# A graph-network layer on one core: the short last chunk of edges summed in the prologue, group 31's x part done there too, and a new order of the last step

## The chip, the cores and the metric

The kernel runs on one core of one Trainium2 chip. The metric is the device time of one execution in microseconds; the median of three runs of the kernel before is 318.07 us (317.57 to 318.27).

## What is computed

```python
agg = segment_sum(edge_attr, dst, num_segments=12500)    # 200000 edges x 128, dst sorted
h = relu(layernorm(x))                                   # 12500 nodes x 128
h = concatenate([h, agg], -1)
h = relu(h @ W1 + b1); h = relu(h @ W2 + b2); h = h @ W3 + b3
out = x + (h - mean(h)) * rsqrt(var(h) + 1e-5) * ln_w + ln_b
```

Everything is float32. The edges alone are 102.4 MB, x and the result 6.4 MB each.

## The kernel before

Edges are sorted by their node. A chunk is 384 edges (3 rows for each of 128 partitions); four chunks are a quad (1536 edges, 768 KB), of which there are 130 (q = 0 to 129). 130 quads leave 320 edges over. They are the short last chunk: it is read as the last 384 edges, and the 64 of them that quad 129 has already counted (`DONE`) are masked out with -1.

For each quad, `seg` (L428) sums the four chunks on PE: 12 matmuls with one-hots of 32 nodes (`onehot`, made for eight chunks at a time by VectorE in `make_onehot`, L876). ScalarE copies the sums from PSUM (`copy_part`, L655), GpSimd makes a placement matrix (`placement`, L795), PE multiplies both (`put`, L444), and VectorE adds the result into `agg` in SBUF at a base read from the data (`add`, L952). Edges come into a ring of eight slots, two loads of 384 KB for each quad, all issued by SP; SP may reload a slot when PE is through with the quad in it (`reload`, L331). Every node group is 384 nodes: groups 0 to 31, and LAST with 212 nodes. A group needs its x part: LayerNorm statistics (`stats_x`, `mean_x`, `scale_x`, `shift_x` on VectorE, `x_sqrt` and `normalise` on ScalarE), three transposes on PE (`transpose_h`), a copy (`copy_ht`); then layer 1 as two matmuls accumulated in one bank (`layer1_x`, `layer1_sums`, the second of which needs the sums), `relu1`, `layer2`, `relu2`, `layer3`; and on VectorE `take_y`, `stats_y`, `mean_y`, `center_y`, `scale_y`, `output`. GpSimd adds the bias into x (`bias_x`).

The order of every engine's instructions is written out by hand. Prologue: dst is loaded, the one-hots' columns are worked out, quads 0 and 1 are summed, group LAST's x part is done, and a flag (L942, L944) decides whether the data fit the windows; while it is worked out PE runs `SPARE` = 20 small matmuls whose results nobody uses (L513). Then every engine branches to `fast`. It does quads 0 to 5 and group 0's x part, and then steps: step i sums four quads (q = 4i + 6 on), does the layers of group i, the x part of group i + 1, and the output of group i - 1. A last step, outside the loops, handles quads 126 to 129, groups 30, 31 and LAST, and the short chunk (L549 to L584 on PE, L738 to L760 on ScalarE, L1089 to L1116 on VectorE). Step 29 does the x part of group 31 too (`more_x`). The x of a group is loaded three steps ahead; results are stored by SP, those of eight groups in parts between the edge loads, those of groups 8 to 29 in pairs behind the last edge load (L328), group 31 by ScalarE's queue (L760), LAST by SP (L315).

## Time and profile before

| | before |
|---|---|
| median of 3 runs | 318.07 us (317.57 to 318.27) |
| the profiled execution | 318.06 us, its span 316.3 us |
| PE busy | 271.3 us, 86% of the span |
| VectorE (DVE) | 248.8 us, 79% |
| GpSimd (POOL) | 168.9 us, 53% |
| ScalarE (ACT) | 149.1 us, 47% |
| DMA | 116.48 MB, mean 368 GB/s |

The span is what the trace covers, from the first instruction to the last; 1.8 us of the execution's time lie outside it. Matmuls are pipelined, so a busy PE is not PE at its peak. "SPq" in a chain is SP's sequencer, which issues the DMAs. All times in the rows are microseconds from the start of the span. A matmul in float32 shows as two records.

### The profile page before, as it was taken

What the parts mean: (1) busy time and instruction counts of PE and PEld (TensorE: products, weight loads), DVE (VectorE), ACT (ScalarE), POOL (GpSimd) and SP (SyncE); (2) the same over time, 40 slices, a digit from 0 to 9 for tenths busy, and PEclk for the clock granted to TensorE, in tenths of its full rate; (3) what the DMA queues carried; (4) which work ended last, traced back from release to release, by engine and by line L of the source; (5) the groups of instructions that cost most, each with busy time, mean ns of one, the idle gap of its engine ahead of it and who ended that gap; (6) DMA issues with size and microseconds to landing.
All of it is one profiled execution on the core that took longest, in us unless ns stands there. A gap on an engine that the chain in (4) does not pass through costs nothing.

```text
span 316.3 us, 12837 instructions
## 1 busy us (share of the span) xinstructions
PE 271.3 (86%) x3967; PEld 185.0 (58%) x3967; DVE 248.8 (79%) x944; ACT 149.1 (47%) x407; POOL 168.9 (53%) x208
## 2 busy tenths in 40 slices
PE   2977999998898888888998888889988888899891
PEld 0654666665565556565665565666655656566460
DVE  4937588988787878878787879788787888877985
ACT  1442555555544445455544444555443545544622
POOL 8626556665545464645545555554446464555431
PEclk9979999999999999999999999999999999999997
DMA  7999999999999999999999999999999999999995
GB/s 246 355 373 372 373 371 372 373 373 373 373 373 373 373 373 373 373 373 373 376 380 378 380 380 379 379 383 379 379 382 378 378 380 383 379 382 381 382 395 180
DMA packets 81854, 116.48 MB, mean 368 GB/s; under 512 B 5712, under 2 KB 81840, under 8 KB 81840
## 3 DMA queue, kind: packets, MB, share of 16 engines
q1 hardware_dynamic: 80826, 115.86, 103.5%
q10 hardware_dynamic: 1014, 0.46, 0.6%
q8 instruction: 6, 0.10, 0.1%
q14 instruction: 8, 0.07, 0.1%
HBM read 109.90 MB, written 6.40 MB: 368 GB/s over the span
## 4 chain that ended last, share of the span: by engine, by line
SPq 52%; PE 16%; issue 13%; DVE 9%; DMA 7%; POOL 1%; DVEq 0%; ACT 0%; POOLq 0%
SPq L296 40%; PE part_ps L439 6%; DMA ring<-in_edge_attr 6%; SPq L323 6%; SPq L291 4%; PE place_ps L450 3%; DVE onehot L880 2%; PE hid_ps L474 2%; PE hid_ps L484 1%; PE hid_ps L467 1%; DMA dst_i<-in_dst 1%; PE y_ps L490 1%; SPq L332 1%; DVE z L999 1%; POOL place L802 1%
## 5 line engine op out<-in xcount | busy, mean ns | idle before, releaser
L802 POOL TENSOR_SCALAR place<-iota,rows_at 128x128 f32<-128x128 f32 x131 | 95.0, 727 | 113.3 <-PE place_ps L450 103.7
L439 PE MATMUL part_ps<-ring,onehot 128*32 128x128 f32 x3120 | 111.9, 277 | 25.7 <-DMA ring<-in_edge_attr 25.7
L439 PEld LDWEIGHTS part_ps<-ring,onehot 128*32 128x32 f32 x3120 | 77.4, 109 | 71.1 <-issue 51.5
L958 DVE TENSOR_TENSOR agg<-place_ps,agg 128x128 f32 x131 | 38.1, 291 | 48.3 <-PE place_ps L450 46.3
L880 DVE TENSOR_TENSOR onehot<-iota,local_t 128x768 f32<-128x768 f32 x66 | 66.2, 1004 | 0.2 <-issue 0.2
L450 PE MATMUL place_ps<-place,part 128*128 128x128 f32 (+1 forms) x262 | 63.6, 325 | 2.7 <-POOL place L802 2.2
L810 POOL TENSOR_TENSOR xs<-xs,vecs 128x384 f32 (+2 forms) x33 | 53.8, 1632 | 19.3 <-ACT h L671 19.3
L657 ACT ACTIVATE part<-part_ps 128x128 f32<-128x128 f32 x131 | 34.8, 267 | 47.0 <-PE part_ps L439 45.1
L450 PEld LDWEIGHTS place_ps<-place,part 128*128 128x128 f32 (+1 forms) x262 | 39.1, 188 | 29.1 <-issue 21.4
L671 ACT ACTIVATE h<-xs,x_shift,x_rstd 128x128 f32 (+2 forms) x98 | 41.3, 483 | 2.4 <-DVE x_shift L873 2.4
L687 ACT ACTIVATE hid<-hid_ps,b1s 128x384 f32<-128x384 f32 (+1 forms) x33 | 19.0, 576 | 44.8 <-PE hid_ps L474 44.8
L1017 DVE SCALAR_TENSOR_TENSOR xs<-z,y_rstd,xs 128x128 f32 (+1 forms) x93 | 31.0, 385 | 4.1
L663 ACT ACTIVATE x_std<-x_mv,eps 128x3 f32<-128x3 f32 (+1 forms) x33 | 9.8, 297 | 42.9 <-DVE x_mv L861 42.9
L490 PE MATMUL y_ps<-w3s,hid 128*128 128x128 f32 x192 | 29.7, 291 | 0.0
L680 ACT ACTIVATE h_t<-ht_ps 128x384 f32<-128x384 f32 x32 | 22.3, 697 | 14.0 <-PE ht_ps L459 14.0
L999 DVE SCALAR_TENSOR_TENSOR z<-y,y_mv,vecs 128x128 f32<-128x128 f32 x96 | 28.4, 348 | 0.1
L484 PE MATMUL hid_ps<-hid,w2s 128*128 128x384 f32 (+1 forms) x66 | 26.8, 487 | 0.5 <-ACT hid L687 0.5
L467 PE MATMUL hid_ps<-h_t,w1x 128*128 128x384 f32 x64 | 26.1, 489 | 0.8 <-ACT h_t L680 0.8
L474 PE MATMUL hid_ps<-agg,w1a 128*128 (+2 forms) x66 | 26.5, 483 | 0.0
L490 PEld LDWEIGHTS y_ps<-w3s,hid 128*128 128x128 f32 x192 | 23.8, 191 | 1.3 <-issue 0.5
L853 DVE BATCH_NORM_STATS2 x_stats<-xs 128x6 f32 (+2 forms) x98 | 22.0, 279 | 0.8 <-DVE flag_i L944 0.8
L983 DVE BATCH_NORM_STATS2 y_stats<-y 128x6 f32<-128x128 f32 x96 | 20.8, 272 | 0.1
(88 smaller groups left out, 206.1 us busy)
## 6 DMA issues: line engine op xcount, KB each, us to landing
ring<-in_edge_attr SPq DMA_DIRECT2D x260, 384.0 KB, 9.0
xs<-in_x SPq DMA_DIRECT2D x32, 192.0 KB, 8.5
out_x<-xs SPq DMA_DIRECT2D x11, 384.0 KB
out_x<-xs SPq DMA_DIRECT2D x16, 72.0 KB
dst_i<-in_dst SPq DMA_DIRECT2D x1, 768.0 KB
out_x<-xs SPq DMA_DIRECT2D x8, 48.0 KB
ring<-in_edge_attr SPq DMA_DIRECT2D x1, 192.0 KB, 8.7
out_x<-xs SPq DMA_DIRECT2D x1, 192.0 KB
```

The costliest lines, as they stand in the source:

```text
L296: sp.dma_start(ring_slot(slot)[:, k * HALF:(k + 1) * HALF, :], half_of_edges(q, k)).then_inc(edges_loaded[slot], 16)
L439: last = nc.tensor.matmul(part_ps[par_q % 2][s * WIN:(s + 1) * WIN, 0:D], onehot[:, oct_par, first + s, j, :], e[:, s, j * D:(j + 1) * D], ...
L450: nc.tensor.matmul(place_ps[par_q % 2][:, 0:P], part[0:rows, par_q % 2, :], place[0:rows, par_q % 2, :], start=True, stop=True).then_inc(p ...
L474: nc.tensor.matmul(hid1_ps[:, 0:n], w1a[:, :], agg[:, bass.ds(g * CHUNK, n)], start=False, stop=True).then_inc(hid1_done, 1)
L490: last = nc.tensor.matmul(y_ps[:, j * D:(j + 1) * D], hid2[:, j, :], w3s[:, :], start=True, stop=True)
L657: nc.scalar.activation(part[0:rows, par_q % 2, :], part_ps[par_q % 2][0:rows, 0:D], ACT.Copy).then_inc(part_copied, 1)
L671: last = nc.scalar.activation(h[0:rows, j, :], xg(g, j), ACT.Relu, bias=x_shift[0:rows, j:j + 1], scale=x_rstd[0:rows, j:j + 1])
L802: nc.gpsimd.tensor_scalar(place[:, par_q % 2, :], iota[:, 0:P], rows_at[:, k:k + 1], None, ALU.is_equal).then_inc(place_ready, 1)
L810: nc.gpsimd.tensor_tensor(v, v, lnbs[0:rows, :].unsqueeze(1).to_broadcast([rows, per, D]), ALU.add).then_inc(x_biased, 1)
L880: nc.vector.tensor_tensor(onehot[:, par % 2, :, :, :], iota[:, 0:WIN].unsqueeze(1).unsqueeze(1).to_broadcast([P, OCT, PER, WIN]), local_t[ ...
L958: nc.vector.tensor_tensor(v, place_ps[par_q % 2][:, 0:P], v, ALU.add).then_inc(added, 1)
L999: last = nc.vector.scalar_tensor_tensor(z_of(g, j), y_of(g, j), y_mv[0:rows, j, 0:1], lnws[0:rows, :], ALU.subtract, ALU.mult)
```

## The change

The short chunk has tiles and semaphores of its own. Its destinations are loaded once more, one edge per element (`tail_i`); its edges go to `tail_e`, behind the first loads of x and ahead of quads 1 to 7. VectorE makes them relative to node 12372 (`TAIL_BASE`), masks the edges that quad 129 counts, and makes a one-hot of 128 nodes for each of its three rows. After the branch PE sums it with three dense matmuls straight into `place_ps[1]`, and VectorE adds it into `agg`. PE waits for that add ahead of quad 2. The separate last segment, copy, placement, put, add and one-hot go.

Group 31 (`TOP`) has its x loaded in the prologue too and its x part done there: statistics ahead of the flag, scale and shift behind it, its three activations on ScalarE ahead of the branch, transposes on PE behind put(0), the copy to `h_top_t` behind copy_part(1), the bias on GpSimd ahead of group 0's. `more_x` goes from step 29.

In the last step the order of PE, ScalarE and VectorE is new; LAST's layer 1 uses the bank `ht_ps`, so it need not wait for the bank of group 31. `SPARE` is 15.

```diff
-SPARE = 20
+SPARE = 15
@@ SP, prologue
+                sp.dma_start(tail_i[:, :], dst[TAIL0:EDGES].rearrange("(p j) -> p j", j=PER)).then_inc(tail_dst_loaded, 16)
...
                 load_x(0, 0, 0)
+                sp.dma_start(xg(TOP), group_rows(x, TOP)).then_inc(top_x_loaded, 16)
                 load_x(1, 1, 0)
+                sp.dma_start(tail_e[:, :, :], edges[TAIL0:EDGES, :].rearrange("(p j) f -> p j f", j=PER)).then_inc(tail_loaded, 16)
@@ SP, end
-                    sp.wait_ge(seg_done, QUADS - RING + 1)
-                    tail = QUADS % RING
-                    sp.dma_start(ring[:, tail, 0:PER * D],
-                                 edges[TAIL0:EDGES, :].rearrange("(p j) f -> p (j f)", j=PER)).then_inc(edges_loaded[tail], 16)
@@ PE
+        def layer1_bank(g):
+            return ht_ps if isinstance(g, int) and g == LAST else hid1_ps
...
                 def fast():
                     pe.wait_ge(wts_loaded, WTS)
+                    pe.wait_ge(tail_loaded, 16)
+                    pe.wait_ge(tail_onehot_ready, 1)
+                    for j in range(PER):
+                        last = nc.tensor.matmul(place_ps[1][:, 0:P], tail_e[:, j, :], tail_onehot[:, j, :],
+                                                start=(j == 0), stop=(j == PER - 1))
+                    last.then_inc(tail_summed, 1)
                     for q in range(AHEAD):
+                        if q == 2:
+                            pe.wait_ge(tail_added, 1)
                         if q >= 2:
                             pe.wait_ge(part_copied, q - 1)
                             seg(q, q, LANDED, q // 2 + 1)
                         if q >= 1:
                             put(q - 1, q - 1, free=q >= 3)
+                        if q == 1:
+                            transpose_h(TOP)
                     transpose_h(0)
...
-                    layer1_x(g)
+                    put(q - 1, q - 1)
+                    layer1(g, q - 1)
                     seg(q, q, loads_of(q), q // 2 + 1)
-                    put(q - 1, q - 1)
-                    layer1_sums(g, q - 1)
+                    layer2(g)
                     put(q, q)
-                    transpose_h(g + 1)
                     seg(q + 1, q + 1, loads_of(q + 1))
-                    layer2(g)
+                    layer1_x(TOP)
                     put(q + 1, q + 1)
-                    layer1_x(g + 1)
                     seg(q + 2, q + 2, loads_of(q + 2), q // 2 + 2)
                     layer3(g)
                     put(q + 2, q + 2)
                     seg(q + 3, q + 3, loads_of(q + 3))
-                    layer1_sums(g + 1, QUADS - 1)
+                    layer1_sums(TOP, QUADS - 1)
                     put(q + 3, q + 3)
-                    slot = QUADS % RING
-                    pe.wait_ge(onehot_ready, QUADS // 2 + 1)
-                    pe.wait_ge(edges_loaded[slot], loads_of(QUADS) - LANDED + 16)
-                    for j in range(PER):
-                        last = nc.tensor.matmul(part_ps[QUADS % 2][0:WIN, 0:D], onehot[:, (QUADS // 2) % 2, 0, j, :],
-                                                ring[:, slot, j * D:(j + 1) * D], start=(j == 0), stop=(j == PER - 1))
-                    last.then_inc(seg_done, 1)
-                    layer2(g + 1)
                     layer1_x(LAST)
-                    put(QUADS, QUADS, rows=WIN)
+                    layer2(TOP)
+                    layer1_sums(LAST, QUADS)
+                    layer3(TOP)
+                    layer2(LAST)
                     layer3_last_bias()
-                    layer3(g + 1)
-                    layer1_sums(LAST, QUADS + 1)
-                    layer2(LAST)
                     layer3_last()
@@ ScalarE
                 x_sqrt(LAST)
                 normalise(LAST)
+                x_sqrt(TOP)
                 copy_ht(LAST)
+                normalise(TOP)
 
                 def fast():
                     act.wait_ge(wts_loaded, WTS)
                     for q in range(2):
                         copy_part(q, q)
+                    copy_ht(TOP)
                     x_sqrt(0)
                     normalise(0)
...
+                    relu1(g)
                     copy_part(q, q)
-                    relu1(g)
-                    copy_ht(g + 1)
+                    relu2(g)
                     copy_part(q + 1, q + 1)
-                    relu2(g)
                     y_sqrt(g - 1)
                     copy_part(q + 2, q + 2)
                     copy_part(q + 3, q + 3)
                     relu1(g + 1)
                     y_sqrt(g)
-                    copy_part(QUADS, QUADS, rows=WIN)
                     relu2(g + 1)
                     relu1(LAST)
                     relu2(LAST)
@@ GpSimd
                     for q in range(2):
                         placement(q, q, q, 1, free=False)
+                    bias_x(TOP)
                     bias_x(0)
@@ VectorE, prologue
                 dve.wait_ge(local_t_ready, ROWT)
+                dve.wait_ge(tail_dst_loaded, 16)
+                nc.vector.tensor_scalar(tail_local[:, :], tail_i[:, :], float(TAIL_BASE), None, ALU.subtract).then_inc(tail_rebased, 1)
                 whole = DONE // PER
-                nc.vector.memset(local_t[0:whole, DONE % PER:PER, CHUNKS:CHUNKS + 1], -1.0)
-                nc.vector.memset(local_t[0:whole + 1, 0:DONE % PER, CHUNKS:CHUNKS + 1], -1.0).then_inc(tail_masked, 1)
+                dve.wait_ge(tail_rebased, 1)
+                nc.vector.memset(tail_local[0:whole, DONE % PER:PER], -1.0)
+                nc.vector.memset(tail_local[0:whole + 1, 0:DONE % PER], -1.0).then_inc(tail_masked, 1)
+                dve.wait_ge(tail_masked, 1)
+                nc.vector.tensor_tensor(tail_onehot[:, :, :], iota[:, 0:P].unsqueeze(1).to_broadcast([P, PER, P]),
+                                        tail_local[:, :].unsqueeze(2).to_broadcast([P, PER, P]), ALU.is_equal
+                                        ).then_inc(tail_onehot_ready, 1)
+                stats_x(TOP, top_x_loaded, 16)
+                mean_x(TOP)
...
+                scale_x(TOP)
+                shift_x(TOP)
...
                     shift_x(0)
                     dve.wait_ge(base_ready, 1)
                     dve.wait_ge(agg_zeroed, 1)
+                    dve.wait_ge(tail_summed, 1)
+                    v = agg[:, TAIL_BASE:NODES]
+                    nc.vector.tensor_tensor(v, place_ps[1][:, 0:P], v, ALU.add).then_inc(tail_added, 1)
+                    dve.wait_ge(tail_added, 1)
                     base = bases(0, AHEAD - 1)
@@ VectorE, last step
                     center_y(g - 1)
-                    make_onehot(q // 2 + 2, 1)
                     add(q + 1, q + 1, base[2])
                     scale_y(g - 1)
                     output(g - 1)
+                    take_y(g)
                     add(q + 2, q + 2, base[3])
-                    take_y(g)
                     stats_y(g)
                     mean_y(g)
+                    add(q + 3, q + 3, base[4])
                     center_y(g)
                     scale_y(g)
-                    add(q + 3, q + 3, base[4])
                     output(g)
-                    add(QUADS, QUADS, base[5])
```

## Rows read from the trace of the kernel before

**Rows 1.** The page: the chain's shares by line; issues of edge loads, us to landing.

```profile
SPq L296 40%; PE part_ps L439 6%; DMA ring<-in_edge_attr 6%; SPq L323 6%; SPq L291 4%; PE place_ps L450 3%; DVE onehot L880 2%; PE hid_ps L474 2%; PE hid_ps L484 1%; PE hid_ps L467 1%; DMA dst_i<-in_dst 1%; PE y_ps L490 1%; SPq L332 1%; DVE z L999 1%; POOL place L802 1%
...
ring<-in_edge_attr SPq DMA_DIRECT2D x260, 384.0 KB, 9.0
```

**Rows 2.** Stretches: us, busy PE, PEld, DVE, ACT, POOL; PE clock, DMA share, GB/s.

```profile
20.00:30.00 10.00, 7.68 (x158) 5.89 (x155) 5.88 (x16) 3.70 (x11) 6.24 (x10) 0.93 1.06 372
240.00:280.00 40.00, 35.39 (x532) 24.07 (x533) 31.62 (x120) 18.29 (x50) 21.27 (x26) 1.00 1.06 380
310.00:317.00 7.00, 0.69 (x4) 0.48 (x4) 2.96 (x13) 1.39 (x6) 1.28 (x3) 0.61 0.32 110
```

**Rows 3.** Timeline of PE, step 29: start, us, instruction, idle before and its releaser.

```profile
285.29 0.86 PE L439 MATMUL part_ps<-ring,onehot 128*32 128x128 f32 x24 [0.93 <-DMA ring<-in_edge_attr]
```

**Rows 4.** Timeline of SP's queue, the last loads and the stores in pairs.

```profile
284.07 0.37 SPq L291 DMA_DIRECT2D xs<-in_x  x1
...
291.27 0.94 SPq L296 DMA_DIRECT2D ring<-in_edge_attr  x2
292.43 0.48 SPq L357 DMA_DIRECT2D ring<-in_edge_attr  x1
292.96 11.00 SPq L328 DMA_DIRECT2D out_x<-xs  x11
```

**Rows 5.** Timeline of the last step up to quad 129: group 31's x part and the tail's one-hot.

```profile
293.81 0.67 DVE L853 BATCH_NORM_STATS2 x_stats<-xs 128x6 f32<-128x128 f32 x3
...
295.71 1.26 ACT L671 ACTIVATE h<-xs,x_shift,x_rstd 128x128 f32<-128x128 f32 x3 [0.44 <-DVE x_shift L873]
...
297.19 0.30 PEld L450 LDWEIGHTS place_ps<-place,part 128*128 128x128 f32 x2 [1.03 <-ACT part L657]
...
300.40 1.04 DVE L880 TENSOR_TENSOR onehot<-iota,local_t 128x768 f32<-128x768 f32 x1
```

**Rows 6.** Timeline from quad 129's segment to VectorE's last instructions.

```profile
302.32 0.86 PE L439 MATMUL part_ps<-ring,onehot 128*32 128x128 f32 x24
...
303.23 0.91 PE L474 MATMUL hid_ps<-agg,w1a 128*128 128x384 f32 x2
...
304.18 0.58 ACT L687 ACTIVATE hid<-hid_ps,b1s 128x384 f32<-128x384 f32 x1 [0.66 <-PE hid_ps L474]
...
304.30 0.84 PE L574 MATMUL part_ps<-ring,onehot 128*32 128x128 f32 x6
...
305.07 0.91 PE L484 MATMUL hid_ps<-hid,w2s 128*128 128x384 f32 x2
...
306.02 0.58 ACT L693 ACTIVATE hid<-hid_ps,b2s 128x384 f32<-128x384 f32 x1 [0.58 <-PE hid_ps L484]
...
307.12 0.94 PE L490 MATMUL y_ps<-w3s,hid 128*128 128x128 f32 x6
...
308.09 0.56 DVE L963 TENSOR_TENSOR y<-y_ps,vecs 128x384 f32<-128x384 f32 x1 [0.91 <-PE y_ps L490]
...
312.46 0.72 DVE L1017 SCALAR_TENSOR_TENSOR xs<-y,y_last_rstd,xs 106x128 f32<-106x128 f32 x2
```

**Rows 7.** Timeline of the prologue: spares, the flag's input, copy_part(0), quad 2, put(2).

```profile
18.91 2.34 PE L513 MATMUL hid_ps<-ident 128*32 128x32 f32 x40
19.15 0.28 DVE L942 TENSOR_REDUCE worst<-place_ps 1x1 f32<-1x128 f32 x1 [2.13 <-PE place_ps L510]
...
20.29 0.45 ACT L657 ACTIVATE part<-part_ps 128x128 f32<-128x128 f32 x2 [1.29 <-DVE flag_i L944]
...
21.78 0.86 PE L439 MATMUL part_ps<-ring,onehot 128*32 128x128 f32 x24
...
26.05 0.46 PE L450 MATMUL place_ps<-place,part 128*128 128x128 f32 x2 [2.20 <-POOL place L802]
```

**Rows 8.** Stretches of 1 us in the prologue, columns as in rows 2.

```profile
18.00:19.00 1.00, 1.00 (x6) 0.62 (x7) 0.00 (x0) 0.36 (x1) 0.72 (x1) 0.51 1.07 373
25.00:26.00 1.00, 0.00 (x0) 0.00 (x0) 0.69 (x2) 0.00 (x0) 1.00 (x2) 1.00 1.06 373
```

## What the change should do, worked out from the rows

> **What bounds the kernel now.** I read the page's chain first: 40% of the span is the SP queue issuing edge loads [rows 1]. Two things can look like that: SP too slow, or SP held back by full DMA queues. The stretches decide it: from 20 us on the DMA share stays at 1.06 and the rate at 372 to 380 GB/s [rows 2], and an edge load lands 9.0 us (median) after its issue [rows 1], far longer than 384 KB at 380 GB/s (1.03 us) takes. So about 9 us of transfers always stand in the queues, and bytes set the pace. PE agrees: deep in the loop it waits 0.93 us for a ring slot once a step [rows 3]; it is close behind, not the limit. The bytes are the same in both kernels but for 1.5 KB. So time can only be won at the end: by when the last quad (q=129) is summed, and by how long the chain behind it is.
>
> At the end the loads are no longer the last thing. Quad 129's two loads are issued from 291.27 to 292.21 [rows 4]; with the median 9.0 us for the second (issued about 291.75) they have landed by about 300.8. PE starts quad 129 at S = 302.32 [rows 6], 1.5 us later. The rows just before tell why: VectorE is full (one-hots, group 31's statistics), ScalarE is busy 1.26 us with group 31's h, so PE waits 1.03 us for a copied part at 297.19 [rows 5]. I call that time "late at S". After S comes a serial chain: sums matmul of group 31 at 303.23, its relu, layer 2 at 305.07 (behind the tail chunk's six matmul records from 304.30), relu 2 at 306.02, layer 3 at 307.12, VectorE's take_y at 308.09, then LayerNorm of group 31 and of LAST in one row on VectorE, whose last instructions run from 312.46 to 313.18 [rows 6]; the last stores take the 3.1 us from there to the end of the span.
>
> **Part 1, bytes ahead of quad 129.** The tail chunk's 192 KB were issued behind quad 129 (292.43 [rows 4]) and now go ahead of all quads but the first: 0.197 MB / 380 GB/s = +0.52 us on its landing. Group 31's x was ahead of it before too (284.07 [rows 4]) and stays ahead: 0. The new load of tail_i is 128 pieces of 12 bytes on SP's queue, ahead of quad 0. No row shows such a load by itself. Lower bound 0 (it hides behind the 768 KB of dst already queued), upper bound 0.48 us, the whole issue of the tail chunk's 128 longer pieces [rows 4]; I take 0.1. The Trainium skill's page "DMA: Bandwidth & Descriptors" (Specifications) puts pieces under 512 B at less than line rate because they are read, modified and written; it gives no time for 128 of them, the sum does not use it. Landing of quad 129: 300.8 + 0.52 + 0.1 = 301.4.
>
> **Part 2, what leaves the last steps.** From VectorE: stats of group 31 0.67, its means about 0.3, two small ones about 0.35, the one-hot for the tail chunk 1.04 [rows 5], one add 0.3: 2.6 us out of a stretch where it was nearly full. From ScalarE: 1.26 for h and a transposed copy of about 0.7. From PE: three transposes and the tail chunk. From GpSimd: one placement. What is late next? Not VectorE (2.6 us of slack against the 1.5 it was behind), but the DMA again: quads arrive every 2.07 us (0.786 MB / 380) and PE needs 1.2 plus one layer, at most 1.9. So quad 129 starts when it has landed or when PE is through layer 3 of group 30, both near 301.4 to 301.6. I take S' = 301.57: 0.75 us earlier than 302.32. Bounds: 0 (PE still late) and 0.9 (start at 301.4).
>
> **Part 3, the chain after S.** Before: take_y at S + 5.77. After, with the same durations: quad 0.79, so group 31's sums at S'+0.81 (the wait for the add of quad 128 that put them at S+0.91 goes); relu 1 0.95 later, as now (303.23 to 304.18): 1.76, ends 2.34; layer 2 at 2.38. Before it came at S+2.75 as the tail chunk stood in front. Now put(129), 0.42, and LAST's x matmul, 0.36, fit before 2.38. Relu 2 at +0.95 (305.07 to 306.02): 3.33, ends 3.91; LAST's sums run meanwhile on PE, done by 3.4, if the add of quad 129 is there: put(129) ends about 1.9, the add 2.2, so 0.8 us of slack. Layer 3 at 3.95, take_y at +0.97: 4.92. That is 0.85 less than 5.77 [rows 6]. From take_y to the end VectorE's order is unchanged (5.09 us, 308.09 to 313.18). LAST must be ready for it: its relu 1 follows relu 2 of group 31, layer 2 follows layer 3, layer 3 of LAST is done about S'+6.6, and VectorE wants it at 4.92 + 2.7 = 7.6: hidden with 1.0 us to spare; if that cover goes, each us later is a us on the end. center_y, scale_y and output of group 30 now stand behind the add of quad 129: 1.9 us on VectorE from S'+2.3, over at 4.2, before take_y at 4.92. The bounds of this part: 0 (some relu or the LAST path late by as much) and 1.2 (relus earlier).
>
> **Part 4, the prologue.** New on VectorE ahead of the flag: rebase, two memsets, a one-hot of 384 elements (half of the 1.04 us for 768), stats 0.67 and means 0.3: about 1.9 us. VectorE idles 2.13 us there before `worst` [rows 7], so the flag moves by 0 to 0.3. After the flag, ScalarE must first make h of TOP: x_sqrt at 19.4, VectorE's scale and shift to 20.0, three activations 1.26 to 21.3. So copy_part(0), at 20.29 before, starts about 21.4. Behind it on ScalarE are queued copy_part(1) and copy_ht(TOP), which waits for PE's put(0) and the transposes (22.7), then x_sqrt(0) about 23.5. VectorE waits for that in scale_x(0), and the tail's add is queued behind: about 24.5. PE waits for the add ahead of quad 2, which thus starts about 24.7 against 21.78 [rows 7]. But before, PE lost 2.20 us at 26.05 waiting for GpSimd's placement [rows 7]; this moves only as far as h of group 0, about 1.7 us, so by quad 4 PE is 1 to 2 us later than now. That costs nothing while the queues are fed. Quads 8 and 9 need only quads 0 and 1; the bytes issued by 24 us (9.6 MB, now 10.0) less those moved (the slices give about 7.8) leave 2.2 MB or 5.8 us of backlog when SP comes to wait for quad 2, done 25.5. SP waits about 1.5 us, the backlog falls to 4 us. The cover is gone only if quad 2 is more than about 5 us late; then each us is one us of the end.
> The five spare matmuls less free 5/20 of 2.34 us = 0.6 us of PE [rows 7], three dense matmuls take it back (0.4 to 1.3 us): nothing, as PE then waits for copy_part(0).
> TensorE's clock: granted 0.51 at 18 us, after PE had stood still from about 15.4 to 18.0, the lower level, 1.2 GHz; yet the idle stretch of 24 to 26 us left it at 1.00 [rows 8]. The new gap (22.8 to 24.7) resembles the second. The Trainium skill, "TensorE: Matmul & The Clock Gate", section "HAM oscillation — how this bites in real kernels", says that an idle PE that waits for its data is throttled again and begins its next work cold. By that rule quads 2 to 5 would run at 1.2 GHz. From rows: twice 0.86 us each, some 3.5 us more PE lag, which by the backlog above still ends near 0 us of cost, at worst 1.
>
> **The sum.** 0.75 (S) + 0.85 (chain) = 1.6 us. The profiled execution took 318.06 us with a span of 316.3, the median is 318.07: 318.06 - 1.6 = 316.5.
>
> **The rivals.**
> *A: only one of the two gains.* For it: landing and PE are near each other at S', and the queues are not empty at the end: 310 to 317 still has a DMA share of 0.32 [rows 2], some 2.2 us of full work, of which the three last stores are only a part. If LAST's stores, now issued at 311.6, find the stores of finished groups in front, they end about 0.8 us later than I say; so too if the loads start 0.8 us later. 318.06 - 0.8 = 317.3, up to 317.8. Against it: SP's last store of two groups is issued by 303.96 [rows 4], 7.6 us ahead.
> *B: slower, the queues run dry in the prologue.* Mechanism: SP cannot reload until quad 2 is summed; ScalarE's copy_part(0) and x_sqrt(0) stand behind TOP, and the cold clock stretches what follows. It decides once SP's wait exceeds the 5.8 us of backlog, less the roughly 2 us in which PE has to get quads 2 to 4 away. If it does, some 3 to 4 us of stream are lost against the 1.6 won: 319.5. For it: a serial loop ScalarE, PE, ScalarE, VectorE, PE that did not exist. Against: 4 us of cover left by my reckoning.
> *C: more is won.* PE may start right on landing and the relus come sooner (bounds 0.9 + 1.2 = 2.1), or quads land sooner than the median says: 315.7.
> *D: nothing changes.* The end is bound by the stream and its stores to the last byte: 318.0. Against: LAST's stores are issued long after the last backlog is thin.
>
> **How the numbers follow.** Forecast (316.1 to 317.1) 0.58; A 0.18; C 0.11; B 0.08; D 0.05. Likeliest: 316.5. The range leaves out B and half of C's far side: 315.5 to 318.1. About 0.2% (0.64 us) is what a measurement can tell from no change: faster than 317.43 is the forecast, C and a third of A: 0.75; slower than 318.71 is B: 0.08; between 0.17.
>
> **What would show it.** Right: quad 129's segment starts 0.6 to 0.9 us earlier and waits for the DMA or for nothing; take_y of group 31 starts 4.7 to 5.2 us behind it; quad 2 starts near 24.7 while the DMA share stays at 1.06 in 20 to 30 us; VectorE's `worst` at 19.1 to 19.5. Wrong: a slice at 20 to 35 us under 370 GB/s (B); the last store landing over 3.2 us after VectorE's last instruction (A); quad 129 starting after 302 with a wait for a part or an add before it (part 2); PE at 0.5 clock beyond 25 us. The prediction fails most easily at part 2, where S' rests on a median landing.

## The result and the profile after

The ratio is 0.9979, 95% interval 0.9969 to 0.9989: 0.7 us faster, 0.35 to 1.0. The forecast was 316.5, 1.6 us faster: the sign was right, the size more than twice too large, and 317.63 lies inside the range.

The page's chain by line answers to [rows 1]:

```profile
SPq L324 46%; DMA ring<-in_edge_attr 6%; SPq L353 6%; PE part_ps L471 5%; SPq L319 5%; PE place_ps L482 2%; DMA dst_i<-in_dst 1%; PE hid_ps L515 1%; PE hid_ps L498 1%; SPq L362 1%; PE hid_ps L505 1%; PE y_ps L521 1%; DVE onehot L916 1%; DVE local L940 1%; DVE least L938 1%
```

SP's issues of edge loads take still more of it, 46% for 40%, and VectorE's one-hots 1% for 2%. The stretches of its trace (us, busy PE, PEld, DVE, ACT, POOL, PE clock, DMA share, GB/s) answer to [rows 2]:

```profile
20.00:30.00 10.00, 6.95 (x126) 5.15 (x129) 5.15 (x17) 4.12 (x14) 6.56 (x10) 1.00 1.06 372
240.00:280.00 40.00, 34.61 (x510) 23.39 (x508) 31.63 (x123) 18.43 (x51) 22.48 (x28) 1.00 1.06 380
310.00:311.00 1.00, 0.00 (x0) 0.00 (x0) 0.85 (x6) 0.67 (x3) 0.10 (x1) 1.00 0.83 298
311.00:312.00 1.00, 0.00 (x0) 0.00 (x0) 0.93 (x5) 0.51 (x3) 1.00 (x3) 0.50 0.42 158
312.00:313.00 1.00, 0.00 (x0) 0.00 (x0) 0.58 (x2) 0.00 (x0) 0.17 (x1) 0.50 0.18 61
```

The stream is as full as before, and the queues are nearly empty when the last stores are issued. The timeline of the prologue answers to [rows 7]: the flag's input, the spares, copy_part(0), quad 2, put(2).

```profile
18.28 1.11 PE L544 MATMUL hid_ps<-ident 128*32 128x32 f32 x30
...
18.53 0.24 DVE L987 TENSOR_REDUCE worst<-place_ps 1x1 f32<-1x128 f32 x1
...
20.55 0.41 ACT L692 ACTIVATE part<-part_ps 128x128 f32<-128x128 f32 x2
...
23.20 0.86 PE L471 MATMUL part_ps<-ring,onehot 128*32 128x128 f32 x24 [1.53 <-DVE agg L1088]
...
26.69 0.46 PE L482 MATMUL place_ps<-place,part 128*128 128x128 f32 x2 [1.41 <-issue]
```

The timeline of the end answers to [rows 3, 4 and 6]: quad 122, the last edge loads on SP, quad 129, and the chain behind it.

```profile
286.75 0.86 PE L471 MATMUL part_ps<-ring,onehot 128*32 128x128 f32 x24 [0.80 <-DMA ring<-in_edge_attr]
...
292.00 1.06 SPq L324 DMA_DIRECT2D ring<-in_edge_attr  x2
...
302.57 0.86 PE L471 MATMUL part_ps<-ring,onehot 128*32 128x128 f32 x24
...
303.36 0.91 PE L505 MATMUL hid_ps<-agg,w1a 128*128 128x384 f32 x2
...
304.31 0.58 ACT L721 ACTIVATE hid<-hid_ps,b1s 128x384 f32<-128x384 f32 x1 [0.54 <-PE hid_ps L505]
...
304.94 0.91 PE L515 MATMUL hid_ps<-hid,w2s 128*128 128x384 f32 x2
...
305.89 0.58 ACT L727 ACTIVATE hid<-hid_ps,b2s 128x384 f32<-128x384 f32 x1 [0.82 <-PE hid_ps L515]
...
306.53 0.94 PE L521 MATMUL y_ps<-w3s,hid 128*128 128x128 f32 x6 [0.31 <-ACT hid L727]
...
307.50 0.56 DVE L1010 TENSOR_TENSOR y<-y_ps,vecs 128x384 f32<-128x384 f32 x1 [0.80 <-PE y_ps L521]
...
311.77 0.81 DVE L1064 SCALAR_TENSOR_TENSOR xs<-y,y_last_rstd,xs 106x128 f32<-106x128 f32 x2
```

What the reader is to see: take_y of group 31 is 4.93 us behind quad 129's start, where the forecast said 4.92, and VectorE's end is 5.08 us behind that. But quad 129 starts at 302.57, not 301.57, which is later than the 302.32 of before. And there is no wait for the DMA at it. The trace also has the landing of each quad's second load. For quad 122, then for quad 129, the view of the line that issues them gives the start of the issue and the time from there to the landing:

```profile
L324 SPq DMA_DIRECT2D ring<-in_edge_attr x1: 939/939/939, 277.2 to 277.2; - x1
DMA to landing us min/median/max: 9.5/9.5/9.5
...
L324 SPq DMA_DIRECT2D ring<-in_edge_attr x1: 597/597/597, 292.5 to 292.5; - x1
DMA to landing us min/median/max: 9.0/9.0/9.0
```

Quad 122 landed at 277.2 + 9.5 = 286.7 and PE began it at 286.75, at once. Quad 129 landed at 292.5 + 9.0 = 301.5, where the forecast said 301.4, and PE came to it 1.1 us later. (In the profile of before the same view gives 291.8 + 8.8 = 300.6 for quad 129, 1.7 us ahead of its start.)

Only two waits of PE show between quad 122 and quad 129: the 0.80 us for quad 122, and 0.55 us for group 30's h_t. That suggested another theory, called T below: the last thing that PE waits for from the stream is quad 122, the first quad of step 29, behind an x load; from there on PE works off what it has. Then bytes ahead of quad 122 cost time and bytes between quads 122 and 129 cost none. Theory R is the forecast's: the landing of quad 129 counts.

### The profile page after: what moved, and what is told of

It reads as the page before. It is cut to its first block, busy times and chain, and to the rows that moved or that the text cites. A ratio compares the mean times of both kernels' runs of the same rounds, so it can differ in the third digit from the quotient of the medians.

```text
span 315.5 us, 12788 instructions
## 1 busy us (share of the span) xinstructions
PE 272.2 (86%) x3955; PEld 184.7 (59%) x3955; DVE 244.4 (77%) x945; ACT 148.9 (47%) x406; POOL 167.5 (53%) x206
## 4 chain that ended last, share of the span: by engine, by line
SPq 59%; issue 13%; PE 12%; DMA 7%; DVE 6%; ACT 1%; DVEq 0%; ACTq 0%
SPq L324 46%; DMA ring<-in_edge_attr 6%; SPq L353 6%; PE part_ps L471 5%; SPq L319 5%; PE place_ps L482 2%; DMA dst_i<-in_dst 1%; PE hid_ps L515 1%; PE hid_ps L498 1%; SPq L362 1%; PE hid_ps L505 1%; PE y_ps L521 1%; DVE onehot L916 1%; DVE local L940 1%; DVE least L938 1%
## 5 line engine op out<-in xcount | busy, mean ns | idle before, releaser
L482 PE MATMUL place_ps<-place,part 128*128 128x128 f32 x260 | 62.9, 324 | 1.7 <-issue 1.4
L844 POOL TENSOR_TENSOR xs<-xs,vecs 128x384 f32 (+2 forms) x33 | 52.5, 1591 | 21.1 <-ACT h L706 21.1
L916 DVE TENSOR_TENSOR onehot<-iota,local_t 128x768 f32<-128x768 f32 x65 | 62.4, 962 | 1.5 <-issue 0.2
L482 PEld LDWEIGHTS place_ps<-place,part 128*128 128x128 f32 x260 | 38.9, 188 | 27.5 <-issue 20.1
L721 ACT ACTIVATE hid<-hid_ps,b1s 128x384 f32<-128x384 f32 x32 | 18.6, 580 | 44.4 <-PE hid_ps L505 44.4
L1064 DVE SCALAR_TENSOR_TENSOR xs<-z,y_rstd,xs 128x128 f32 (+1 forms) x93 | 27.9, 353 | 6.5 <-DVE y_rstd L1054 6.4
L714 ACT ACTIVATE h_t<-ht_ps 128x384 f32<-128x384 f32 x31 | 21.6, 696 | 13.6 <-PE ht_ps L491 13.6
L515 PE MATMUL hid_ps<-hid,w2s 128*128 128x384 f32 (+1 forms) x66 | 26.7, 486 | 0.1
L505 PE MATMUL hid_ps<-agg,w1a 128*128 (+1 forms) x64 | 26.0, 488 | 0.0
L498 PE MATMUL hid_ps<-h_t,w1x 128*128 128x384 f32 x62 | 25.2, 489 | 0.6 <-ACT h_t L714 0.6
```

What stands on the lines that cost most here:

```text
L482: nc.tensor.matmul(place_ps[par_q % 2][:, 0:P], part[0:rows, par_q % 2, :], place[0:rows, par_q % 2, :], start=True, stop=True).then_inc(p ...
L505: nc.tensor.matmul(layer1_bank(g)[:, 0:n], w1a[:, :], agg[:, bass.ds(g * CHUNK, n)], start=False, stop=True).then_inc(hid1_done, 1)
L515: nc.tensor.matmul(hid2_ps[:, 0:n], w2s[:, :], hid1[:, 0:n], start=True, stop=True).then_inc(hid2_done, 1)
L844: nc.gpsimd.tensor_tensor(v, v, lnbs[0:rows, :].unsqueeze(1).to_broadcast([rows, per, D]), ALU.add).then_inc(x_biased, 1)
L916: nc.vector.tensor_tensor(onehot[:, par % 2, :, :, :], iota[:, 0:WIN].unsqueeze(1).unsqueeze(1).to_broadcast([P, OCT, PER, WIN]), local_t[ ...
```

## Landmarks of all the profiles

The columns, in us: start of quad 122 (it waits for the DMA in every kernel), from there to the start of quad 129, from there to take_y of group 31, VectorE's end, and from that to the end of the span. The last columns are the median, and the ratio to the kernel before on the same chip with its interval.

| kernel | quad 122 | to 129 | to take_y | DVE end | to span end | median | ratio |
|---|---|---|---|---|---|---|---|
| before | 285.29 | 17.03 | 5.77 | 313.18 | 3.1 | 318.04 | |
| e11 before again | 286.19 | 16.35 | 5.71 | 313.34 | 3.4 | 318.19 | 1.0005 (0.9992 to 1.0018) |
| e1 before, x31 early | 286.07 | 16.36 | 5.72 | 313.23 | 3.1 | 318.79 | 1.0017 (1.0003 to 1.0030) |
| e10 before, x31 behind q4 | 285.78 | 16.34 | 5.74 | 312.94 | 3.1 | 318.89 | 1.0025 (1.0012 to 1.0038) |
| e6 before, both early | 286.63 | 16.35 | 5.71 | 313.78 | 3.3 | 320.31 | 1.0061 (1.0041 to 1.0081) |
| the changed kernel | 286.75 | 15.82 | 4.93 | 312.58 | 2.9 | 317.63 | 0.9979 (0.9969 to 0.9989) |
| e2 no tail_i load | 286.66 | 15.79 | 4.93 | 312.46 | 3.2 | 317.46 | 0.9980 (0.9965 to 0.9996) |
| e4 parts behind | 286.90 | 15.80 | 4.93 | 312.71 | 3.2 | 317.61 | 0.9990 (0.9974 to 1.0006) |
| e9 loads later | 286.92 | 15.79 | 4.94 | 312.73 | 3.0 | 317.64 | 0.9991 (0.9977 to 1.0005) |
| e3 stored early 6 | 286.17 | 15.79 | 4.94 | 311.98 | 3.9 | 317.76 | 0.9987 (0.9971 to 1.0003) |
| e8 stored early 7 | 287.30 | 15.79 | 4.93 | 313.11 | 3.3 | 317.41 | 0.9975 (0.9962 to 0.9988) |
| e12 stores between | 286.61 | 15.79 | 4.93 | 312.42 | 3.6 | 317.75 | 0.9981 (0.9962 to 1.0000) |
| e5 x31 late | 287.00 | 16.58 | 5.22 | 313.88 | 2.9 | 318.38 | 1.0001 (0.9986 to 1.0017) |
| e7 spare 100 | 288.97 | 15.79 | 4.94 | 314.78 | 2.8 | 319.71 | 1.0047 (1.0024 to 1.0070) |

The columns "to 129" and "to take_y" repeat to 0.06 us in kernels with the same code there, but for the 17.03 of before, to which e11 comes back. The column "quad 122" does not: it differs by 0.9 us between the two executions of the kernel before. The eight kernels with the change's own last step need 15.8 us from quad 122 to quad 129, whatever is in the stream.

## The experiments

**e1: group 31's x moved into the prologue, alone.**

```diff
+                sp.dma_start(xg(GROUPS - 1), group_rows(x, GROUPS - 1)).then_inc(top_x_loaded, 16)
                 load_x(1, 1, 0)
...
-                            stats_x(i + 2, x_loaded[par], 16 * pairs + 32)
+                            stats_x(i + 2, top_x_loaded, 16)
```

> The kernel before with one edit: group 31's x (192 KB) is loaded in the prologue instead of between quads 125 and 126. Theory T (what sets the start of quad 129 is the landing of quad 122, the last one PE waits for, plus PE's and VectorE's own work): every first quad of a step lands 0.52 us later (0.197 MB / 380 GB/s), quad 122 starts near 285.8 instead of 285.29, and the time rises by 0.3 to 0.5 us. Theory R (the forecast's: only the bytes ahead of quad 129 count, and they are the same): quad 129 lands as before, the time is the same within 0.1 us.

Measured: 1.0017 (1.0003 to 1.0030), 0.5 us slower (0.1 to 1.0). The forecast gave this edit the price 0; the low end of the interval only just excludes that, and e10 below excludes it clearly. The profile's quad 122 agrees in direction only, since its 0.78 us contain the spread of the stream. Early in the stream the price is seen better: quad 7 lands at 26.2 us in both profiles of the kernel before, at 26.7 here, at 26.9 in e10. The same load further back in the prologue (**e10**, behind quad 4) costs 0.8 us (0.4 to 1.2), no less:

> The kernel before with group 31's x loaded in the prologue, behind quad 4, where the earlier experiment had it ahead of quad 1. Theory H: without the hole it costs its bytes only, 0.52 us on every quad behind it (deep in the loop 141.3 against 140.8; the earlier placement gave 141.60 in its profile), and the time is 318.4 to 318.6. If any added load in the prologue costs 0.8 us or more wherever it stands, the time is 318.8 or more as there.

**e4: three stores taken out from between quads 122 and 129.**

```diff
-                    step(2 * t + 1, 1, t, g, {0: 0, 3: 1})
-                    step(2 * t + 2, 0, t + 1, g, {2: 2}, more_x=False)
+                    step(2 * t + 1, 1, t)
+                    step(2 * t + 2, 0, t + 1, more_x=False)
+                    for k in range(len(OUT_PARTS)):
+                        store_part(g, k)
```

> The changed kernel with the three stores of group 7 moved from between the loads of quads 122 and 129 to behind quad 129. Only bytes between those two quads move. Theory T: quad 122 lands as in the changed kernel (286.75), quad 129 starts as there (302.57, within 0.15), the time is the same within 0.1 us. Theory R: quad 129 starts 0.52 us earlier and the time falls by 0.5 us.

Measured: the same time (317.61 against 317.63). The rows of PE, quad 122 and quad 129:

```profile
286.90 0.86 PE L473 MATMUL part_ps<-ring,onehot 128*32 128x128 f32 x24 [0.97 <-DMA ring<-in_edge_attr]
...
302.70 0.86 PE L473 MATMUL part_ps<-ring,onehot 128*32 128x128 f32 x24
```

15.80 us apart, as in the changed kernel, though 197 KB fewer stand ahead of quad 129. Quad 129 had landed at 301.3, 1.4 us ahead of its start. That is what T says and R denies.

**e3, e8: two groups' stores, or one, behind the last edge load.** The edit is `STORED_EARLY` = 6, or 7, for 8.

> The changed kernel with STORED_EARLY = 6: the stores of two groups (393 KB) go behind the last edge load instead of into the stream. Theory T: quad 122 lands 1.03 us earlier (near 285.7), quad 129 starts 1.0 us earlier (near 301.55), and VectorE ends 1.0 us earlier; the stores then drain 1.0 us later, near 312.3, so the end gains only 0.5 to 1.0 us: 316.7 to 317.1 us. If the end were bound by the drain of the stores already, the time would not fall. If PE's lag from the prologue were the limit, quad 122 would not move.

> The changed kernel with STORED_EARLY = 7: one group's store leaves the stream. With 6 quad 122 came 0.58 us earlier and VectorE ended 0.60 us earlier, yet the drain of the stores, full until 311.0 and at 0.7 of share until 313.0, held the last stores. With 7: quad 122 near 286.45, VectorE's end near 312.3, and the drain ends near 312.3. If VectorE's end and the drain both bound the end, this lies between: 317.3 to 317.6, at best 0.3 us under the changed kernel; if only the chain bound it, 6 would have gained 0.6 us, which it did not.

With 6, VectorE ends at 311.98, 0.6 us earlier than in the changed kernel, and none of it arrives: 317.76. The 1 us stretches of e3's end, against those of the changed kernel above:

```profile
310.00:311.00 1.00, 0.00 (x0) 0.00 (x0) 0.81 (x6) 0.90 (x4) 0.70 (x2) 1.00 1.03 384
311.00:312.00 1.00, 0.00 (x0) 0.00 (x0) 0.95 (x4) 0.00 (x0) 0.57 (x2) 1.00 0.70 250
312.00:313.00 1.00, 0.00 (x0) 0.00 (x0) 0.00 (x0) 0.00 (x0) 0.00 (x0) 0.95 0.74 262
```

The queues are full until 311, and from VectorE's end to the end of the span it takes 3.9 us instead of 2.9: LAST's stores find others in front. With 7 the time is 317.41, which its interval does not set apart from the changed kernel. The two groups' stores also took only 0.6 us off quad 122's start in the profile, where 393 KB at 380 GB/s would be 1.03.

That price was too high, as the trace of before shows without any experiment. Between quads 50 and 58 no store stands in the stream, between quads 114 and 122 the three parts of one group do. PE waits for the stream at each of the four. The starts of quads 50 and 114, to be read with the 140.81 of quad 58 and the 285.29 of quad 122:

```profile
122.89 0.86 PE L439 MATMUL part_ps<-ring,onehot 128*32 128x128 f32 x24 [1.00 <-DMA ring<-in_edge_attr]
...
267.22 0.86 PE L439 MATMUL part_ps<-ring,onehot 128*32 128x128 f32 x24 [0.94 <-DMA ring<-in_edge_attr]
```

17.92 us without the stores, 18.07 with them. From quad 74 to quad 122, with six groups stored, eight quads take 18.09 us in the mean. So a group's 197 KB among the loads cost 0.15 to 0.17 us, a third of the 0.52 that they would take at 380 GB/s; the rate of the stream is 380 GB/s with the stores in it and 372 without [rows 2]. Two groups' stores are worth 0.3 to 0.4 us, not 1.03. From quad 58 to quad 122, which takes out what the early stream loses in one execution and not in another, it is 144.3 to 144.6 us in the eleven profiles with eight groups stored early 144.1 in e3 and e8, 144.3 in e12 below: less by a few tenths, as two stores or one would be, and not by 1.0.

**e12: the same two groups' stores moved between quads 125 and 128**, where T says that they are free.

```diff
+                    step(2 * t + 1, 1, t)
+                    store(IN_PARTS)
+                    store(IN_PARTS + 1)
...
+                        if k == 1:
+                            store(IN_PARTS + 2)
```

> The changed kernel with the stores of groups 5, 6 and 7 issued between the loads of quads 125 and 128, where PE is behind the stream anyway; the other five stay in parts ahead of quad 122, and the order behind quad 129 is unchanged. Two groups' stores (393 KB) thus leave the stream ahead of quad 122 without coming behind quad 129. Theory T: quad 122 starts 0.6 to 1.0 us earlier than the changed kernel's 286.8 (mean of four profiles), near 286.0; quad 129 lands up to 1.0 us later after it but PE needs 15.8 us to reach it in any case, so it starts near 301.9; the drain ends where it does in the changed kernel; the time falls by 0.4 to 0.7 us, to 316.9 to 317.2. Theory R (bytes ahead of quad 129 set the end): quad 129 starts as in the changed kernel, 317.6. If the later landing of quads 126 to 129 takes PE's slack of 0.8 us, the gain is under 0.3 us and PE waits for a ring slot after quad 125.

Half right. 590 KB now stand between quads 122 and 129 and PE still takes 15.79 us with no wait for a ring slot: T's main claim holds. Quad 129 lands at 302.0 and starts at 302.40, so 0.4 us of its cover are left. But the gain did not come: 317.75. Quad 122 started at 286.61, 0.2 us earlier than the mean of the changed kernel's four profiles and not 0.6 to 1.0: two groups' stores out of the stream are worth 0.3 to 0.4 us, as reckoned above. And the last stores took 3.6 us, against 2.9 to 3.2 in those four, with a DMA share of 0.98, 0.62 and 0.38 from 310 to 313 us. That the drain of the stores took back what was left is likely; one profile does not show it, and e3 shortens the chain and lengthens the drain at once.

T has a limit. In the changed kernel quad 125 lands at 283.6 + 9.5 = 293.1 and starts at 293.10, with nothing to spare, while quads 126 to 129 land 1.1 to 1.7 us ahead of their starts. The stores of e12 were put behind the loads of quad 125. Bytes ahead of that quad were not tried and would hardly be free.

**e2: no load of tail_i; e9: the two new loads later.** In e2 a memset stands for the load. In e9 group 31's x stands behind quad 2 and the short chunk's edges behind quad 4:

```diff
                 for q in range(1, RING):
                     load_quad(q, q)
+                    if q == 2:
+                        sp.dma_start(xg(TOP), group_rows(x, TOP)).then_inc(top_x_loaded, 16)
+                    if q == 4:
+                        sp.dma_start(tail_e[:, :, :], edges[TAIL0:EDGES, :].rearrange("(p j) f -> p j f", j=PER)).then_inc(tail_loaded, 16)
```

> The changed kernel without the load of tail_i (128 pieces of 12 bytes); the tile is filled by a memset instead, so the short chunk is summed into the wrong node. If this load is what holds the stream back by the 0.3 us that bytes do not explain (first quads of a step start 1.35 us later than before, 1.03 us of it are the two 192 KB loads), they start 0.3 us earlier than in the changed kernel (near 141.85 instead of 142.16) and the time falls by 0.3 us. If the load is hidden behind dst, as the forecast had it (0.1 us), nothing moves by more than 0.1 us.

> The changed kernel with its two new 192 KB loads issued later in the prologue: group 31's x behind quad 2, the short chunk's edges behind quad 4. The bytes ahead of quad 122 are the same. Theory H: beyond their bytes (1.03 us) the early loads cost the stream a hole near 13 to 15 us, in which the DMA share falls to 0.8 to 0.9 while SP is held up in an issue; with the loads later the hole is gone (share 1.05 or more in every us from 12 to 20), quads deep in the loop start near 141.85 and the time falls by 0.3 to 0.6 us, to 317.0 to 317.3. If only bytes count, the quads start as in the changed kernel's profile (142.1 to 142.3) and the time stays at 317.6.

Neither moved the time (317.46 and 317.64) nor quad 122 by more than 0.2 us. So the 128 small pieces cost nothing that can be seen, and theory H, a loss by the place of the loads, is not borne out: e9 has no hole (share 1.05 or more from 12 to 18 us) and starts deep in the loop at 142.50, no earlier. What remained of the 1.35 us is taken up by the next run.

**e11: the kernel before once more.**

> The kernel before once more, unchanged, for the spread of its profile and its time. All theories: the ratio is 1.000 within 0.002. If the profile of before is typical, there is no hole in the DMA share at 12 to 16 us and quads deep in the loop start at 140.8 within 0.2; if holes come and go in every kernel, they start up to 1 us later and part of the 1.35 us that the changed kernel's are late is no effect of the change.

The ratio is 1.0005. Quad 58 in the profile of before, then in that of e11:

```profile
140.81 0.86 PE L439 MATMUL part_ps<-ring,onehot 128*32 128x128 f32 x24 [1.00 <-DMA ring<-in_edge_attr]
```

```profile
141.88 0.86 PE L439 MATMUL part_ps<-ring,onehot 128*32 128x128 f32 x24 [0.98 <-DMA ring<-in_edge_attr]
```

The same code, 1.07 us apart, though e11 has no hole at 12 to 16 us either. The landings tell where it arose: quad 7 lands at 26.2 us in both, quad 10 0.4 us later in e11, quad 22 at 60.1 in before and 61.1 in e11. So the stream gains or loses up to 1 us between 26 and 61 us, and the 1.35 us cannot be told from its 1.03 us of bytes and this spread. A second thing differs. VectorE's one-hot of step 29, in before and in e11:

```profile
292.13 1.75 DVE L880 TENSOR_TENSOR onehot<-iota,local_t 128x768 f32<-128x768 f32 x1
```

```profile
293.00 0.95 DVE L880 TENSOR_TENSOR onehot<-iota,local_t 128x768 f32<-128x768 f32 x1
```

In before it ran beside GpSimd's bias_x and took 0.8 us longer. In e11 it ran beside it too, and there GpSimd took 0.8 us longer. The bias in before, then in e11:

```profile
292.05 1.02 POOL L810 TENSOR_TENSOR xs<-xs,vecs 128x384 f32 x1 [0.28 <-ACT h L671]
```

```profile
292.95 1.85 POOL L810 TENSOR_TENSOR xs<-xs,vecs 128x384 f32 x1 [0.31 <-ACT h L671]
```

 From quad 122 to quad 129 it takes 17.03 us there and 16.34 to 16.36 in the four other profiles of this code. So 0.7 us of what [rows 5] show as "VectorE is full" belongs to that one execution. In the changed kernel the same pair meets, and there too GpSimd pays:

```profile
293.51 1.85 POOL L844 TENSOR_TENSOR xs<-xs,vecs 128x384 f32 x1 [0.31 <-ACT h L706]
293.56 0.94 DVE L916 TENSOR_TENSOR onehot<-iota,local_t 128x768 f32<-128x768 f32 x1
```

That the two engines got into each other's way is my reading of the times, one of the two 0.8 us longer each time they meet; no run kept them apart.

**e5: the changed kernel with group 31's x part late again.**

```diff
                     layer2(g)
                     put(q, q)
+                    transpose_h(TOP)
                     seg(q + 1, q + 1, loads_of(q + 1))
...
-                    step(STEPS - 2, 1, (STEPS - 2) // 2)
+                    step(STEPS - 2, 1, (STEPS - 2) // 2, more_x=True)
```

> The changed kernel with its second part undone: group 31's x is loaded in step 28 again, its x part is done by VectorE and ScalarE in step 29, its transposes and copy in the last step; the short chunk stays in the prologue and the last step keeps its new order. Theory T: first quads of a step start 0.5 to 0.8 us earlier than in the changed kernel (near 141.5), quad 122 near 286.1. From there to quad 129 it takes between 16.2 us (PE's 15.8 and three transposes) and the 17.0 of the kernel before: quad 129 starts between 302.3 and 303.1, the chain behind it is the changed kernel's 4.93 us to take_y, and the time is 317.3 to 318.2. If moving group 31's x part is what pays, the time is above the changed kernel's 317.6 by 0.3 us or more; if its bytes cost what its work saves, the two are the same.

318.38, ratio 1.0001 (0.9986 to 1.0017): the short chunk in the prologue and the new order alone win nothing that can be told from zero; with group 31's x part moved too it is 0.9979. Theory T's numbers were missed here: quad 122 started at 287.00, not near 286.1, quad 129 at 303.58, to take_y it took 5.22 and not 4.93, and the time is above the 317.3 to 318.2 stated. Part of the difference shows in the columns: 16.58 and 5.22 against 15.8 and 4.93, 1.1 us, less the 0.5 of its bytes. Why the stream was late, and why to take_y is 0.3 longer here, stays open.

**e6: both loads early, nothing else.**

```diff
+                sp.dma_start(xg(GROUPS - 1), group_rows(x, GROUPS - 1)).then_inc(top_x_loaded, 16)
                 load_x(1, 1, 0)
+                sp.dma_start(tail_e[:, :, :], edges[TAIL0:EDGES, :].rearrange("(p j) f -> p j f", j=PER)).then_inc(tail_loaded, 16)
```

> The kernel before with both 192 KB loads (group 31's x, the short chunk's edges) issued in the prologue where the change has them, and nothing else moved. Theory T: quad 122 starts where the changed kernel has it (286.5 to 286.9 against 285.29), and the time rises by 1.0 to 1.4 us, to 319.1 to 319.5; so the change's other parts together save 1.5 to 1.9 us, what the forecast said, and the place of the loads takes back 1.0 or more. If the loads' place costs little, the time stays below 318.6 and the forecast's savings were too large instead.

1.0061 (1.0041 to 1.0081): 1.3 to 2.6 us slower, from six executions, of which the profiled one was the fastest (318.86 against 319.85 to 320.41). More than the 1.03 us of bytes; the profile, 286.63 at quad 122, does not show the rest. Direction and order agree with T, the surplus stays open; so the price of early bytes is known in time only roughly (0.5, 0.8, and 1.3 to 2.6 us for two loads).

**e7: quad 2 five us later.** The edit is `SPARE` = 100.

> The changed kernel with SPARE = 100: 170 more small matmul records (37 ns each in the changed kernel's profile, 6.3 us) ahead of the branch, so quad 2 starts 4 to 6 us later than the 23.20 us of the changed kernel. By the forecast's reckoning of 5.8 us of queued transfers, SP's waits for quads 2 to 4 are still covered: the DMA share stays at 1.06 in 24 to 34 us, the first quads of a step deep in the loop start as before (142.2), and the time is the same within 0.2 us. By the rival that the queues run dry, there is a hole in the share at 26 to 34 us, and each us of it is one us of the time: 318.5 or more.

```profile
28.17 0.86 PE L471 MATMUL part_ps<-ring,onehot 128*32 128x128 f32 x24 [1.52 <-DVE agg L1088]
```

```profile
29.00:30.00 1.00, 1.00 (x30) 0.85 (x26) 0.50 (x2) 0.38 (x2) 0.75 (x1) 1.00 0.90 315
30.00:31.00 1.00, 0.24 (x12) 0.00 (x0) 1.00 (x1) 0.28 (x1) 1.00 (x2) 1.00 0.93 247
31.00:40.00 9.00, 8.36 (x140) 5.63 (x140) 4.79 (x17) 2.90 (x8) 4.33 (x8) 1.00 1.03 355
```

The rival was right here. Quad 2 came 5.0 us later than in the changed kernel, the queues ran partly dry from 29 us on (355 GB/s for nine us where 372 is normal), quad 122 came 2.2 us later and the time rose by 2.1 us to 319.71. The cover is about 5.0 - 2.2 = 2.8 us for this kernel, an estimate, with the spread of quad 122's start in it; the backlog in bytes came to 5.8 us, and rival B, which took 2 us off it, was nearer with 3.8. The bytes do not account for all of it: from 29 to 40 us e7 moves 342 GB/s where the changed kernel moves 372, 0.33 MB or 0.9 us of stream, while quad 58 comes 2.5 us later. Backlog counted in bytes over all 16 engines is too kind; what became of the other 1.6 us is not shown.

More of the change, by code:

```diff
@@ L45 @@
 DONE = CHUNKS * CHUNK - TAIL0
+TAIL_BASE = NODES - P
 OCT = 2 * QC
@@ L48 @@
 LAST = GROUPS
+TOP = GROUPS - 1
 LAST0 = GROUPS * CHUNK
@@ L98, in gnn_kernel @@
         place = sb("place", [P, 2, P])
+        tail_e = sb("tail_e", [P, PER, D])
+        tail_i = sb("tail_i", [P, PER], I32)
+        tail_local = sb("tail_local", [P, PER])
+        tail_onehot = sb("tail_onehot", [P, PER, P])
         iota = sb("iota", [P, BANK])
@@ L245, in nth, with transposed @@
         def nth(g):
-            return 1 if isinstance(g, int) and g == LAST else g + 2
+            if isinstance(g, int) and g >= TOP:
+                return 1 if g == LAST else 2
+            return g + 3
+        def transposed(g):
+            if isinstance(g, int) and g >= TOP:
+                return h_last_t if g == LAST else h_top_t
+            return h_t
+        def layer1_bank(g):
+            return ht_ps if isinstance(g, int) and g == LAST else hid1_ps
         def group_rows(t, g):
@@ L465, in layer1_x @@
                     pe.wait_ge(ht_ready, nth(g))
-                    t = h_t if n == CHUNK else h_last_t
-                    nc.tensor.matmul(hid1_ps[:, 0:n], w1x[:, :], t[:, :], start=True, stop=False)
+                    nc.tensor.matmul(layer1_bank(g)[:, 0:n], w1x[:, :], transposed(g)[:, :], start=True, stop=False)
                 def layer1_sums(g, sums=None):
@@ L714, in fast, with step @@
                     copy_ht(0)
-                    def step(i, first=False, more_x=False):
+                    def step(i, first=False):
                         q = 4 * i + AHEAD
@@ L763, in general @@
                     act.wait_ge(wts_loaded, WTS)
-                    with act.Fori(0, GROUPS) as g:
+                    copy_ht(TOP)
+                    with act.Fori(0, TOP) as g:
                         x_sqrt(g)
@@ L771, in general @@
                         y_sqrt(g)
-                    relu1(LAST)
-                    relu2(LAST)
-                    y_sqrt(LAST)
+                    for g in (TOP, LAST):
+                        relu1(g)
+                        relu2(g)
+                        y_sqrt(g)
                 branch(act, fast, general)
@@ L840, in general @@
                 def general():
-                    with pool.Fori(0, GROUPS) as g:
+                    bias_x(TOP)
+                    with pool.Fori(0, TOP) as g:
                         bias_x(g)
@@ L1046, in fast, with step @@
                     add(4, 4, base[4])
-                    def step(i, par, pairs, first=False, more_x=False):
+                    def step(i, par, pairs, first=False):
                         make_onehot(2 * i + 4, 0)
@@ L1162, in group @@
                         finish(g)
-                    with dve.Fori(0, GROUPS // 2) as t:
+                    with dve.Fori(0, TOP // 2) as t:
                         group(2 * t, 0, t)
                         group(2 * t + 1, 1, t)
+                    group(TOP - 1, 0, TOP // 2)
+                    finish(TOP)
                     finish(LAST)
```

60 lines of the change are left out of this document (34 added, 26 removed).

## The prediction, point by point

**Part 2 failed, and with it the sum.** "What is late next? Not VectorE, but the DMA again": wrong. The landing of quad 129 came where the forecast had it, 301.5 for 301.4; that PE would be there to meet it did not. From quad 122 on PE needs 15.8 us to reach quad 129 (seven segments of 0.79, seven placements of 0.42, the layers, the wait for h_t), while the stream needs 301.5 - 286.7 = 14.8: taking stores out ahead of it (e4) or putting more in (e12) changes nothing. The term that was mis-sized is PE's time for a quad, "1.2 plus one layer, at most 1.9" against the 2.07 of the stream. The starts of quads 122 to 129 lie 2.51, 1.86, 1.98, 3.88, 1.85, 1.86 and 1.88 us apart: the 3.88 hold the transposes of group 30, the 0.55 us wait for its h_t and both matmuls of its layer 1. And PE is late already at the start of the stretch, as it waits for quad 122; it has to be compared with the stream over the whole stretch. S' came out as 302.57 for 301.57, and that 1.0 us is what the forecast's 1.6 had too much.

**Part 1: right in bytes, wrong in place.** The short chunk's 0.52 us fits its bytes. "Group 31's x stays ahead: 0" is right for quad 129 and wrong for quad 122, behind which it used to stand: another 0.52 us by its bytes. e1 and e10 price it at 0.5 and 0.8 us. The load of tail_i costs nothing visible (e2: 317.46 against 317.63). The Trainium skill, "DMA: Bandwidth & Descriptors" (Specifications), has pieces under 512 B below line rate; no row here shows that for the 128 pieces of tail_i.

**"Late at S" by 1.5 us** was read from one execution, in which 0.7 us were its own. What the removed work and the new order gave back between quads 122 and 129 is 16.35 - 15.80 = 0.55 us. The forecast had the lateness fall from 1.5 us to under 0.2.

**Part 3 was right**: 4.93 for 4.92, and 5.08 to VectorE's end.

**Part 4**: the flag came no later (`worst` at 18.53, before 19.15), quad 2 started at 23.20, earlier than the 24.7 forecast, because copy_part(0) began at 20.55, not 21.4. The cost of nothing is consistent with the changed kernel's full stream, and the cover was overrated (e7). TensorE's clock was granted in full in this profile from 20 to 24 us, 2.4 GHz (first row); in e4, whose prologue is the same code, it was at 0.50, that is 1.2 GHz (second):

```profile
20.00:24.00 4.00, 2.36 (x36) 1.73 (x35) 1.56 (x9) 2.81 (x9) 2.10 (x3) 1.00 1.06 373
```

```profile
20.00:24.00 4.00, 2.69 (x11) 2.30 (x11) 1.40 (x9) 1.96 (x8) 2.19 (x4) 0.50 1.06 374
```

In e4 it stayed there until 30 us, quads 2 to 4 took 1.5 us each for 0.86, quad 2 came 1.0 us later (24.23), and the time was the same (317.61 against 317.63). But it fell at 20 us, ahead of the gap of which the forecast spoke and behind PE's stillness from 16.0 to 17.9. In e2 it was full until 24.6, behind that gap (PE stood from 21.7 to 23.2), and then 0.50 until 31 us, again at no cost in time (317.46). The rule of the Trainium skill, "TensorE: Matmul & The Clock Gate", section "HAM oscillation — how this bites in real kernels", that an idle PE begins its next work cold, thus fits e2 and not the changed kernel's own profile.

**The rivals.** A, only one of the two gains, is what happened (317.3 was its time): the chain gained 0.8 us, S' nothing. Its own reasons, late loads or stores in front of LAST's, are not what took S' away. Whether the forecast's 316.5 would have come with S' at 301.57 was not tested: VectorE would have ended at 311.6, where the changed kernel's DMA share is still 0.42, and in e3, which ends at 312.0 with more stores behind it, the last stores took 3.9 us instead of 2.9. B did not happen, but decides at about 2.8 us. C is out. D was wrong for this kernel; whether it holds for a further shortening of the chain is open for the same reason.

**The sum by what was measured**: bytes ahead of quad 122 +1.03, from there to quad 129 -0.55, to take_y -0.8, the rest 0: -0.3 us. The medians differ by 0.41, the ratio says 0.7 (0.35 to 1.0). The mean start of quad 122 is 286.81 in the four profiles with the changed kernel's bytes ahead of it (changed kernel, e2, e4, e9) and 285.74 in the two of before, 1.07 apart, as the bytes say; but the two of before are 0.9 apart themselves, so this agreement is in part luck. e1 and e10, with one load more than before, have 285.93 in the mean, only 0.2 later.

## What to carry to other kernels

When a full stream feeds an engine that is nearly as slow, find the last item for which the engine still waits, and read from the trace when the items behind it landed and when they were used: loads moved ahead of that item cost about their transfer time, bytes moved behind it cost nothing until that cover (here 1.1 us at quad 129) or the drain at the end is the limit. Price a store among loads by the trace and not by its bytes: here it cost a third of them. Before a stall of less than a us is counted as a gain, take a second profile of the same kernel: here two of them differed by 1.1 us in the stream and by 0.7 us in the stretch on which the sum stood. And price the drain: a shorter chain can pay only down to the moment when the last transfer ahead of the final store has gone. How near this kernel is to that was not measured.

## What was not expected of the hardware

The stream's loss in the prologue varies from run to run: by 24 us it had moved 7.80 MB in before, 7.72 in e11 and 7.67 to 7.74 in the kernels with the new prologue. The 0.08 MB between before and e11 are 0.2 us, where quads deep in the loop are 1.07 us apart; so the bytes moved and the landings tell different things, and the rest came later than 26 us. In several of the new prologues the DMA share fell near 13 to 15 us (0.90 in the changed kernel, 0.81 in e5, 0.76 in e7) while a single issue of SP took 1.4, 2.1 and 3.1 us; in before and e11 the share did not fall. e9 had no such fall and was no faster. What makes it stays open.
